# An attention and feed-forward layer on 8 cores: row normalisation on GpSimd, another order of the first two chunks, f's transposes and weight loads spread over later stages

## What is computed

```
x = x + attn(layernorm(x))       # f = layernorm(x) W^T + b
                                 # e = f f^T + bias(|i-j|),  a = softmax(e) f
x = x + layernorm(x) Q^T * scale # Q = clip(round(weight / scale), -1, 1)
                                 # scale = max(mean|weight|, 1e-5)
bias(d) = min(d, 10) * 0.01;  layernorm: (x - mean) / sqrt(var + 1e-5)
```

## Time and profile before

| | |
|---|---|
| median of 3 runs | 984.45 us (983.73 to 987.19) |
| profiled execution | 982.92 us, its slowest span 981.4 (core 1) |
| spans of the cores | 973.0 to 981.4 us, clock 0.986 to 0.991 |
| busy share | TensorE 96%, VectorE 57%, ScalarE 34%, GpSimd 32% |
| chain that ended last | TensorE 72%, VectorE 10%, DMA 10%, ScalarE 2% |
| costliest groups | L466 240.9 us, L794 463.2 us, L856 90.4 us, L402 63.3 us, all TensorE matmuls |
| VectorE | L500 81.5 us in 128 (mean 637 ns), L504 78.2 us in 127 |

### The profile page before, as it was taken

The page is one execution under the profiler, slowest core; times in us unless marked ns, Lnnn a source line. Parts: engine busy times, 40 slices in busy tenths (PEclk is TensorE's granted clock), DMA queues, the critical chain, the costliest instruction groups (busy, mean ns, idle before and its releaser), DMA issues.

```text
span 981.4 us, 15321 instructions; the slowest of 8 cores (973.0 to 981.4 us)
## 1 busy us (share of the span) xinstructions
PE 941.5 (96%) x4821; PEld 461.4 (47%) x4821; DVE 564.1 (57%) x858; ACT 336.8 (34%) x479; POOL 310.9 (32%) x334
## 2 busy tenths in 40 slices
PE   7898979979999999899999999999999999999998
PEld 6654424434444444544444444444444444444443
DVE  5655668888886678633343344444445555566643
ACT  4555633333333344353434232231311313223110
POOL 4010112222222233101012124235336456576760
PEclk9999979989999999999999999999999999999999
DMA  8477896986675349889579799999999987878522
GB/s 265 164 181 198 241 220 171 228 211 191 167 220 155 123 159 210 271 226 261 158 220 239 200 236 237 205 221 244 197 213 220 213 244 178 239 179 206 139 56 75
DMA packets 230074, 195.81 MB, mean 200 GB/s; under 512 B 136910, under 2 KB 200682, under 8 KB 228074
## 3 DMA queue, kind: packets, MB, share of 16 engines
q1 hardware_dynamic: 146170, 79.99, 36.6%
q10 hardware_dynamic: 68432, 63.44, 26.3%
q0 software_dynamic: 15392, 51.40, 16.5%
HBM read 108.79 MB, written 53.49 MB: 165 GB/s over the span
## 4 chain that ended last, share of the span: by engine, by line
PE 72%; DVE 10%; DMA 10%; SPq 3%; issue 2%; ACT 2%; DVEq 0%; ACTq 0%; POOLq 0%
PE pb L794 39%; PE pb L466 15%; PE pb L856 10%; PE pb L402 5%; DMA ln2T<-ln 5%; DVE rm L500 2%; DMA xe<-x 2%; SPq L300 2%; DVE cmax L504 2%; PE pt L284 2%; DVE st L321 1%; DVE st L323 1%; DVE lnb L348 1%; DMA escr<-er 1%; DMA ln1Ta<-lnb 1%
## 5 line engine op out<-in xcount | busy, mean ns | idle before, releaser
L466 PE MATMUL pb<-fT 128*128 128x512 bf16 (+3 forms) x1152 | 240.9, 366 | 11.3 <-ACT fT L412 6.4
L794 PE MATMUL pb<-f,pTb 128*128 128x512 bf16 x1024 | 233.0, 380 | 0.0
L794 PE MATMUL pb<-f,pTa 128*128 128x512 bf16 x1024 | 230.2, 379 | 0.0
L466 PEld LDWEIGHTS pb<-fT 128*128 128x128 bf16 x1152 | 110.9, 99 | 132.2 <-issue 16.8
L507 POOL DMA_DIRECT2D escr<-er x128 | 71.7, 563 | 270.0 <-DVE er L497 133.5
L794 PEld LDWEIGHTS pb<-f,pTa 128*128 128x128 bf16 x1024 | 99.8, 99 | 114.1
L794 PEld LDWEIGHTS pb<-f,pTb 128*128 128x128 bf16 x1024 | 99.9, 99 | 111.6
L806 DVE SCALAR_TENSOR_TENSOR o<-pb,st,xres 128x512 f32<-128x512 f32 x64 | 48.1, 751 | 141.2 <-PE pb L794 139.5
L747 POOL TENSOR_TENSOR acc<-acc 128x128 f32<-128x128 f32 (+6 forms) x90 | 108.7, 1208 | 13.2 <-POOL acc L747 0.4
L492 ACT COPY er<-pb 128x512 f32<-128x512 f32 (+2 forms) x128 | 69.9, 546 | 123.5 <-PE pb L466 64.6
L500 DVE TENSOR_REDUCE rm<-er 128x1 f32<-128x512 f32 (+2 forms) x128 | 81.5, 637 | 36.6 <-ACT er L492 25.4
(11 more groups left out here) (107 smaller groups left out, 706.5 us busy)
## 6 DMA issues: line engine op xcount, KB each, us to landing
escr<-er POOLq DMA_DIRECT2D x105, 256.0 KB, 3.4
xres<-x POOLq DMA_DIRECT2D x32, 512.0 KB, 9.5
out<-outb SPq DMA_DIRECT2D x31, 512.0 KB, 7.2
xb<-x SPq DMA_DIRECT2D x28, 512.0 KB, 6.3
wst<-wt SPq DMA_DIRECT2D x8, 512.0 KB, 14.3
wst<-ft SPq DMA_DIRECT2D x8, 512.0 KB, 6.8
escr<-eB POOLq DMA_DIRECT2D x15, 256.0 KB, 2.9
eB<-escr ACTq DMA_DIRECT2D x2, 1920.0 KB, 11.5
```

What stands on the lines that cost most here:

```text
L466: inst = e.matmul(bk[:, 0:n], fT[:, h * S + I * P:h * S + (I + 1) * P], fT[:, h * S + c0:h * S + c0 + n], start=(h == 0), stop=(h == NH - 1))
L794: inst = e.matmul(bank[bav[nb]][:, :], pT[I % 2][:, j * P:(j + 1) * P], f_sb[:, j * D + nb * 512:j * D + (nb + 1) * 512], start=(pos == 0) ...
```

## The change

`ln_apply` goes from VectorE to GpSimd, and `ln_stats` waits in turn for the application that read its column of moments. A first Ln activation on a constant stands at the start of ScalarE's queue. Weight casts go to VectorE (0, 1, 3, 5) and GpSimd (2, 4, 6, 7). The sequence before stage 1 has another order: chunk 0's projections for h = 3 to 7 are done in one piece, and the normalisations of chunk 1 stand ahead of the transposes. The stages place the standard deviations and normalisations later and wider apart, spread loads, absolute sums and quantisations, and do the f transposes of chunk 1 in stage 3, 2 in stage 4, 3 and 4 in stage 5, 5 and 6 in stage 6. Chunk 0's stay where they are, and so do chunk 7's in stage 7. At the start of the second phase the maxima of `cmax` are folded some positions later. In `egroup_out` the store is issued ahead of the column maximum in program order; they are in different queues.

```diff
+        ACT.op(lambda e, w: e.activation(
+            col(STD), col(EPSC), AF.Ln, bias=col(EPSC), scale=1.0), t_eps)
...
-            mom_tok[s] = ln_moments(xbuf(s), s % 4, x_tok[s])
+            mom_tok[s] = ln_moments(xbuf(s), s % 4, x_tok[s],
+                                    apply_tok.get(s - 4))
...
-            apply_tok[s] = DVE.op(lambda e, w: e.tensor_scalar(
+            apply_tok[s] = POOL.op(
+                lambda e, w: e.tensor_scalar(
...
-            if h in (0, 2):
-                cast_tok[h] = ACT.op(lambda e, w: e.copy(
-                    WT[:, h * D:(h + 1) * D], wst[h][:, :]), sl_w[h].tok)
-                return
-            cast_tok[h] = POOL.op(lambda e, w: e.tensor_copy(
+            cast_tok[h] = (DVE if h in (0, 1, 3, 5) else POOL).op(lambda e, w: e.tensor_copy(
...
-        for h in (1, 3, 4, 5, 6, 7):
-            w_cast(h)
...
-        warm(9)
+        warm(7)
         ln_stats(2)
         ln_rs(2)
-        w_cast(0)
         ln_done(1)
         warm(4)
         ln_stats(3)
         ln_rs(3)
+        w_cast(0)
+        w_cast(1)
         fproj(0, 0, 0)
         ln_done(2, DVE)
+        fproj(0, 1, 0)
+        ln_apply(3)
         w_cast(2)
-        fproj(0, 1, 0)
+        xtrans(3, DVE)
+        w_cast(3)
         fproj(0, 2, 0)
-        ln_done(3, DVE)
-        for u, h in ((0, 3), (1, 0), (1, 1), (0, 4), (1, 2), (0, 5), (1, 3),
-                     (0, 6), (1, 4)):
-            fproj(0, h, u)
+        fproj(0, 0, 1)
+        fproj(0, 1, 1)
+        w_cast(4)
+        w_cast(5)
+        w_cast(6)
+        w_cast(7)
+        fproj(0, 2, 1)
+        for h in (3, 4, 5, 6, 7):
+            fproj(0, h)
         emit_band()
         late = []
         ln_stats(4)
         ln_rs(4)
+        ln_apply(4)
         ln_stats(5)
-        fproj(0, 5, 1)
-        fproj(0, 7, 0)
         ln_rs(5)
-        fproj(0, 6, 1)
-        ln_done(4)
-        fproj(0, 7, 1)
+        ln_apply(5)
         ln_stats(6)
         egroup(0, 0, late)
         egroup(1, 0, late)
-        ln_done(5)
+        xtrans(4)
         ln_rs(6)
+        ln_apply(6)
         ln_stats(7)
         egroup(2, 0, late)
+        xtrans(5)
         ln_rs(7)
-        ln_done(6)
+        ln_apply(7)
         egroup(3, 0, late)
         fproj(1, 0, 0)
+        xtrans(6)
         fproj(1, 1, 0)
-        ln_done(7)
+        xtrans(7)
         for k in range(4):
             ln_stats(8 + k)
         todo0 = {
-            0: [late[0]], 1: [late[1]], 5: [lambda: ln_rs(8, 4)],
-            6: [lambda: ln_apply(8), lambda: ln_apply(9)], 7: [late[2]],
-            9: [lambda: xtrans(8), lambda: xtrans(9), lambda: ln_apply(10)],
-            10: [late[3]], 11: [lambda: ln_apply(11)],
-            12: [lambda: xtrans(10)], 13: [lambda: xtrans(11)],
+            0: [late[0]], 1: [late[1]], 4: [lambda: ln_rs(8, 4)],
+            5: [lambda: ln_apply(8), lambda: ln_apply(9)], 6: [late[2]],
+            7: [lambda: xtrans(8), lambda: ln_apply(10)],
+            8: [lambda: xtrans(9), lambda: ln_apply(11)], 9: [late[3]],
+            11: [lambda: xtrans(10)], 12: [lambda: xtrans(11)],
         }
...
                 if c == 1:
-                    when = [0, 1, 2, 3, 5, 6, 7, 9, 10]
+                    when = [0, 1, 2, 3, 5, 6, 7, 9, 11]
...
                     when = [int(n * v) for v in (
-                        0, .06, .12, .18, .25, .31, .38, .45, .52)]
+                        0, .06, .12, .18, .3, .34, .41, .48, .55)]
...
-            if c == 2:
-                for k in range(3, NH):
-                    at_slot(2 * k - 6, lambda k=k: ft_load(k))
-                for k in range(NH):
-                    at_slot(4 + 2 * k, lambda k=k: absum(k))
-                at_slot(n - 1, scale_sum)
+            for c_, i, fn, k in (
+                    (1, 9, ft_load, 0), (1, 12, ft_load, 1),
+                    (1, 15, ft_load, 2), (2, 0, ft_load, 3),
+                    (2, 4, ft_load, 4), (2, 8, ft_load, 5),
+                    (2, 12, ft_load, 6), (2, 16, ft_load, 7),
+                    (2, 4, absum, 0), (2, 8, absum, 1), (2, 12, absum, 2),
+                    (2, 16, absum, 3), (3, 1, absum, 4), (3, 4, absum, 5),
+                    (3, 10, absum, 6), (3, 12, absum, 7),
+                    (3, 17, quant, 0), (3, 20, quant, 1), (4, 5, quant, 2),
+                    (4, 9, quant, 3), (4, 19, quant, 4), (4, 23, quant, 5),
+                    (5, 20, quant, 6), (5, 25, quant, 7)):
...
             if c == 3:
-                at_slot(1, scale_prep)
-            for c_, i, k in ((3, 3, 0), (3, 6, 1), (3, 13, 2), (3, 19, 3),
-                             (4, 4, 4), (4, 18, 5), (5, 4, 6), (5, 20, 7)):
...
+                at_slot(13, scale_sum)
+                at_slot(15, scale_prep)
+
+            fts = [(k, h) for k in {3: (1,), 4: (2,), 5: (3, 4),
+                                    6: (5, 6)}.get(c, ())
+                   for h in range(NH)]
+            for i, (k, h) in enumerate(fts):
+                at_slot(int(n * (i + .7) / len(fts)),
+                        lambda k=k, h=h: ftrans(k, h))
             if c < NCH - 1:
-                for h in range(NH):
-                    v = (.6 + .05 * h if c < 4 or h > 3 else .02 + .07 * h)
-                    at_slot(int(n * v), lambda h=h: ftrans(c, h))
...
-                    at_mark(0, 4, lambda: (mfin_col(nn, last_cm[0]),
-                                           mfin_tmp(nn)))
-                    at_mark(0, 6, lambda: mfin_col(nn - 1, last_cm[0]))
+                    at_mark(0, 10, lambda: (mfin_col(nn, last_cm[0]),
+                                            mfin_tmp(nn)))
+                    at_mark(0, 14, lambda: mfin_col(nn - 1, last_cm[0]))
                     for g, pos in zip(range(6, -1, -1),
-                                      (8, 12, 16, 20, 24, 32, 40)):
+                                      (16, 19, 22, 25, 31, 36, 41)):
```

More of the change, by code:

```diff
@@ L236, in build_nc @@
                 cmax[:, i * 512:(i + 1) * 512], -3.0e38))
-        DVE.op(lambda e, w: e.memset(col(EPSC), EPS))
+        t_eps = DVE.op(lambda e, w: e.memset(col(EPSC), EPS))
         DVE.op(lambda e, w: e.memset(col(ZERO), 0.0))
@@ L444, in build_nc @@
         er_count = [0]
-        er_free = [(None, None)] * NER
+        er_free = [()] * NER
         store_toks = {}
         nq_of = {}
-        e_last_dve = {}
+        e_last_cm = {}
         e_last_pe = [None]
@@ L501, in egroup_out @@
                 rm[:, I * 9 + q:I * 9 + q + 1], dst, AXX), ta)
[L502 to L506, removed]
             ts = POOL.dma(slot, lambda e, w: e.dma_start(
@@ L509, in egroup_out @@
             store_toks.setdefault(I, []).append(ts)
+            m = n - P if q == 0 else n
+            if m:
+                tm = e_last_cm[I] = DVE.op(lambda e, w: e.tensor_tensor(
+                    cmax[:, c0:c0 + m], cmax[:, c0:c0 + m], dst[:, 0:m],
+                    ALU.max), t_cm0)
             if I < NST - 2:
@@ L1086, in stage @@
                     when = [int(n * v) for v in (
-                        0, .06, .12, .18, .25, .31, .38, .45, .52)]
+                        0, .06, .12, .18, .3, .34, .41, .48, .55)]
                 for k in range(4):
                     at_slot(when[k], lambda k=k: ln_stats(s0 + k))
+                at_slot(when[4], lambda: ln_rs(s0, 4))
+                for k in range(4):
                     at_slot(when[5 + k], lambda k=k: ln_apply(s0 + k))
@@ L1092, in stage @@
                         at_slot(when[5 + k], lambda k=k: xtrans(s0 + k))
-                at_slot(when[4], lambda: ln_rs(s0, 4))
-            if c == 1:
-                for k in range(3):
-                    at_slot(9 + 3 * k, lambda k=k: ft_load(k))
-            if c == 2:
-                for k in range(3, NH):
-                    at_slot(2 * k - 6, lambda k=k: ft_load(k))
-                for k in range(NH):
-                    at_slot(4 + 2 * k, lambda k=k: absum(k))
-                at_slot(n - 1, scale_sum)
-            if c == 3:
-                at_slot(1, scale_prep)
-            for c_, i, k in ((3, 3, 0), (3, 6, 1), (3, 13, 2), (3, 19, 3),
-                             (4, 4, 4), (4, 18, 5), (5, 4, 6), (5, 20, 7)):
-                if c == c_:
-                    at_slot(i, lambda k=k: quant(k))
+            for c_, i, fn, k in (
[9 more added lines that the diff above has]
+                    (5, 20, quant, 6), (5, 25, quant, 7)):
+                if c == c_:
+                    at_slot(i, lambda fn=fn, k=k: fn(k))
+            if c == 3:
+                at_slot(13, scale_sum)
[6 more added lines that the diff above has]
+                        lambda k=k, h=h: ftrans(k, h))
             if c < NCH - 1:
-                for h in range(NH):
-                    v = (.6 + .05 * h if c < 4 or h > 3 else .02 + .07 * h)
-                    at_slot(int(n * v), lambda h=h: ftrans(c, h))
                 if c == NCH - 2:
@@ L1121, in stage @@
                     at_slot(9 + 3 * g, lambda g=g: ptrans31(g))
```

(2 more changed lines are left out.)

7 lines of the change are left out of this document (3 added, 4 removed).

## The result

The changed kernel took 1009.31 us in the median of 4 runs (1008.38 to 1010.19), the kernel before beside it 984.09: a ratio of 1.0259, with a 95% interval of 1.0218 to 1.0300. The forecast was 962, with a range of 955 to 974. It is slower by 25 us where 22 less was expected.

A forecast was written before the change was run, and what follows sets the result against it. TensorE's work plus its pauses was taken as the bound. On core 5, 5.1 - 0.3 + 4.7 + 8.9 + 1.3 = 19.7 us off 978.5 gave 958.8; two steps of 1.5 made 962, range 955 to 974.

The forecast's parts named there:

- the price of a normalisation on GpSimd: Per strip on GpSimd: 1.2 us in the start, 1.7 later, 2.4 at most, taken from a cast of the same size.
- The start: Before stage 1: fproj(1,0,0) at about 37.8 us instead of 41.9, stage 1 near 56.5; gain 5.1 us, bounds 2 and 6.
- Stage 1's wait stays: Stage 1: TensorE's 3.5 us wait for chunk 3's first normalised strip stays; loss 0.3 us, range 0 to 2.
- Stage 2: End of stage 2: the pause from late stores goes; gain 10.4 us on core 1, 4.7 on core 5.
- the ring's 9.6: Stage 2: four er buffers give about 9.6 us, so some 5 us of GpSimd's hold on stores is covered.
- the pause of 10.4: End of stage 2, core 1: TensorE's 6.4 us wait plus 4.0 us at the slow clock, both expected to go.
- Stage 4: Start of stage 4: VectorE no longer behind, so TensorE's wait goes; gain 6.7 us on core 1, 8.9 on core 5.
- the risk that I had priced at nothing: scale_prep, a TensorE matmul, waits for scale_sum on VectorE: no loss expected, as VectorE would not be behind.
- The second phase: Start of second phase: mfin_col(29)'s 3.9 us wait falls to 2.6; gain 1.3 us, range 0 to 3.
- The fourth: Rival, stages 2 to 5: GpSimd holds stores beyond the ring, each costing a 10.4 us pause; 1004 us, chance 0.04.
- rival 1: Stage 2: GpSimd's hold outlasts the ring, so core 1's pause stays; 968.6, then above 972 us; chance 0.15.
- rival 2: Stages 3 to 5: GpSimd's work slows VectorE's cmax maxima, a pause moves to stage 5; 970 us, chance 0.10.

The follow-up runs named there:

- e2: Changed kernel with GpSimd's normalisation replaced by a plain cast of the same strip, subtraction and scaling left out: 968.5 us, ratio 0.9843.
- e1: Changed kernel with one line back, the normalisation on VectorE: 980.7 us, ratio 0.9987.
- e6: e1 with the weight casts on the engines of the kernel before, new order of chunks 0 and 1 kept: 983.5 us profiled, 979.2 in another execution.
- e11: Changed kernel with stores of egroups other than a row's first issued from ScalarE's queue instead of GpSimd's: 998.2 us in one execution.
- e9: e2 with stage 2's standard deviation and applications at the slots of the kernel before: 968.9 us, ratio 0.9879.
- e5: e1 with the order and weight casts up to stage 1 as in the kernel before: 974.2 us, ratio 0.993.
- e4: Kernel before with seven GpSimd operations on scratch (a memset, six forms of tensor_scalar) in its idle time behind the casts: 984.74 us in one execution.
- e10: e5 with chunk 4 transposed by TensorE and stage 3's quantisations, scale_sum, scale_prep, stage 1's standard deviations and mfin_col moved: 974.7 us, ratio 0.9924.
- e12: e5 with the slots of moments, standard deviations and applications and the maxima's positions as in the kernel before: 977.7 us, ratio 0.998.

## Why the prediction was wrong

The step that failed is one term of the sum, the price of a normalisation on GpSimd. Of the 47 us between forecast and measurement it is 41: e2, which has the same places and waits at 1.08 us a strip, took 41 us less than the changed kernel at 3.8. The sum had "GpSimd's normalisation 1.2", later 1.7, with 2.4 as the upper end; it was 3.8. The other 6 to 7 us are a gain in the stages that was too large even at the assumed price (e2: 968.5 for 962).

Two steps led to the price. The nearest row for the cost was a cast of the same shape and types, and I took shape and types for what makes two operations alike. And the upper end came from a GpSimd operation held up by VectorE: contention around the cast, not another price of the instruction. The two-input additions on GpSimd in the trace of before, at 1.9 ns a column, would have been the farther row; even that one was short of 3.8. Groups by form, core 1:

```profile
L737 POOL TENSOR_TENSOR acc<-pTa 128x1024 f32<-128x1024 bf16 x1 | 2.1, 2113 | 7.3 <-PE pb L756 7.3
```

Point by point:

- *The start.* Mechanism and size right at the assumed price (37.7 and 56.6 in e2), wrong at the true one: 80.9 against a forecast 56.5. Four strips of 3.8 us in a row are longer than the 1.9 us a strip that the moments set, and they became the pace. The clock at its lower level for 13.7 us or more was not in the sum either. That the new order is good only with a second, quick engine was not seen: on VectorE it costs 6 us (e1), 4 of them by its order alone (e6).
- *Stage 1's wait stays.* Right: 3.6 at the assumed price, 6.4 at the true one, 2.9 more than before for 3.0 more of work.
- *Stage 2.* The hold on the stores' queue was named, with 5 us as the point from which it decides. It decided at less: e11 shows 8 us for it over all stages. The 5 us had been worked out with 3.4 us for a store to land, the median of the whole run. At the very place of the pause, core 1 of the kernel before from 120 to 134 us, the median is 8.2:

```profile
escr<-er POOLq DMA_DIRECT2D x4, 256.0 KB, 8.2
```

With that, 0.9 us is left of the ring's 9.6. And at the assumed price the pause of 10.4 did not go but moved, in part to the transposes of chunk 4 at the start of stage 3 (e2, e9). I had looked at who waits behind the hold, not at who needs the last strip that the later slots delay.
- *Stage 4.* VectorE's balance held: no wait of 5 us at the start of stage 4 in e1, e2 or e5. In e1 and e5 2.7 to 6.9 us came back at scale_prep, the risk that I had priced at nothing since "VectorE is then not behind". It was not behind with work; in e1's row it stood 2.5 us at the lnb buffer.
- *The second phase.* 2.9 for a forecast 2.6.
- *The rivals.* The fourth had the right sign and the right mechanism for the stages, with a chance of 0.04. That its 1004 us lies near 1009 is luck: it had four pauses of 10.4 us for the stores, where e11 shows 8 us in all, and nothing for the start, where 20 of the 25 us are. For the start I had no rival above the cost bound. The range ended at 974, because the bound of the one unknown price did.
- *Small slips in the sums.* 1.2 - 0.8 is 0.4, not 0.3, and rival 1's 968.6 and two steps of 1.5 make 971.6, not above 972. Neither matters here.
- *VectorE gets nothing back* (rival 2). It got most of it back: its column maxima took 4.8 to 7.9 us more on the eight cores, 7.7 on core 4, for 26 of normalisation given away. And the loss did not grow with the price: with e2's casts the maxima took 85.2 us on core 0, for 83.0 on that core with normalisations. The timeline shows why; core 4 of the changed kernel:

```profile
231.11 3.78 POOL L352 TENSOR_SCALAR lnb<-xb,st 128x1024 bf16<-128x1024 f32 x1
...
231.61 1.24 DVE L507 TENSOR_TENSOR cmax<-cmax,er 128x512 f32<-128x512 f32 x1
...
233.75 0.69 DVE L507 TENSOR_TENSOR cmax<-cmax,er 128x512 f32<-128x512 f32 x1
```

A maximum that begins 0.5 us into a normalisation takes 1.24 us in place of 0.69, one that begins 2.6 us into it takes 0.69. Over all cores 132 maxima began 1.4 us or more into a normalisation, and none was longer than alone. The Trainium skill warns, in Perfetto Trace Analysis, Optimizing Scalar/DVE Operations, that moving work between the two might not help, as they share a read port. The traces agree that they hold each other, and show here a hold of the first 1.05 us or so of GpSimd's operation (0.50 + 0.55 in this row; elsewhere 0.35 more for one begun at 0.70), not of its 3.8.
- *The price.* The Trainium skill says, in GPSIMD Engine Reference, Engine selection, that one-input operations run there at roughly line rate. e4 agrees for the cast (1.04 us) and not for tensor_scalar (3.0 to 3.9).

The stages take 323 to 326 us in e1, e2, e5, e9, e10 and e12 alike, whichever pause is taken away, and most of that is TensorE's own work. Its matmuls in the stages come to about 309 us at full rate: an estimate from 1.73 us for 8 of 512 columns, for 167 such groups, the narrow ones and the transposes of one chunk. TensorE's waits there sum to 9.8 to 11.5 us in these six, by the median over the cores, and the 3 to 6 us that are left are about what TensorE's time at its lower clock costs. So the stages can give some 15 us more at most. What stays open is why the waits always sum to some 10 us; only e9 and e10 followed a pause to the next one.

The best of these kernels that compute everything are e5 and e10, equal within the noise: 974.2 for 980.7 us (0.993) and 974.7 for 982.0 (0.992). Both have the new stages with the old start and the normalisation on VectorE. It is a gain of 0.7 to 0.8%.

## What to carry to other kernels

When an operation moves to an engine on which the trace does not show that very instruction, a row of the same shape is no bound: measure it first in that engine's idle time. Even the dearest row of that size in the trace, 2.1 us for a two-input addition, would have been short of 3.8. Count the strips that stand in a row on the new engine, not only the one: the start lost 20 us, as 3.8 is twice the pace of the moments in front of it. Where a bound rests on how fast a DMA lands, read it in the stretch in question: 8.2 us there for 3.4 over the run. A pause taken away in a schedule as full as this one is worth its length only until the next late step; here six different schedules of the same stages came out within 3 us.

## What the runs showed of the hardware

On GpSimd tensor_scalar over 128x1024 from f32 took 3.78 us with two operations and 3.0 to 3.1 with one, whether the scalars were constants or a column, and whether bf16 or f32 was written (e4); a cast of the same size took 1.04. VectorE did the first in 0.81. Beside GpSimd's tensor_scalar VectorE's two-input maximum of 512 columns, 0.69 alone, took 1.24 when it began 0.5 us into it, 1.04 at 0.7, and 0.69 from 1.4 us on; beside a cast it took 1.15 at 0.46. VectorE's one-input reductions kept their mean of 637 ns. Stores of 256 KB issued from GpSimd's queue landed after 3.4 us in the median of the kernel before, and after 8.2 in a stretch of 14 us in which the core's DMA engines moved 271 GB/s, for 200 over the whole span.
